# Graph and mixture-of-experts network on one Trainium2 core: TensorE turns the next group's rows ahead of this group's logits

## The chip, the cores and the metric

The kernel runs on 1 core of a Trainium2 chip. The metric is the device time of one execution in microseconds; of several runs the median is given. The engines are named as in the profile: PE is TensorE's matmul side and PEld its weight loads, DVE is VectorE, ACT is ScalarE, POOL is GpSimd, SP is SyncE.

## The reference

Two layers, each a graph attention network beside a mixing network, and then a feed-forward network of experts, on 6250 rows of 256 features with 106,250 edges, all in float32. The change lies in the last step, the feed-forward network of the second layer:

```python
x = x + _L1_ffn_ref(_layernorm(x, axis=-1)[None], L1_ffn_W1, L1_ffn_b1, L1_ffn_Wg, L1_ffn_bg, L1_ffn_Wd, L1_ffn_bd)[0]

def _L1_ffn_ref(x, W1, b1, Wg, bg, Wd, bd):      # C = 256, HID = 1024, E = 8
    H = jax.nn.gelu(xf @ W1 + b1, approximate=False)
    probs = jax.nn.softmax((H @ Wg + bg) / TEMP, axis=-1)
    assign = jnp.argmax(probs, axis=-1)
    for e in range(Wd.shape[0]):
        y = H @ Wd[e] + bd[e]
        sel = (assign == e)[:, None]
        out = out + jnp.where(sel, probs[:, e:e + 1] * y, 0.0)
```

So every row gets a hidden vector H (1024 wide), eight logits out of it, and the output of the one expert with the largest logit.

## The kernel before

The kernel is written engine by engine: each engine has its own queue of instructions in a fixed order, and the queues meet only in semaphores. Three graph stages ("layers" in the kernel's own count, the third being the second half of the second graph network) take most of the time. Behind the third come the two stages of the last feed-forward network:

- **Routing** (`route_tensor`, `route_scalar`, `route_vector`, `route_gpsimd`, `route_sync`). The 6250 rows lie in SBUF as 49 blocks of 128, the last one padded. They are taken in 13 groups (`GROUPS`): twelve of four blocks and one of a single block. For each group the kernel computes H for all rows only to get the logits, chooses the expert, counts the place of each row in its expert's list, and GpSimd writes the rows to a table in HBM, sorted by expert (`D_sx`).
- **Experts** (`ffn1_tensor` and its siblings). Rows come back from that table in 15 groups, 14 of them full, are turned (L2505), go through W1 (L2513) and through their expert's matrix (L2494).

TensorE wants its left operand with the contraction on the partitions, so rows must be turned (transposed) before a matmul with W1, and the logits, which come out as 8 x 512, must be turned back to rows x 8 before VectorE can take a maximum over eight experts.

The routing is a pipeline over rounds r = 0 to 14. In round r, PE's queue holds, in this order:

1. L2203: the hidden layer of group g = r - 1. Eight slices of 128 hidden units, two matmuls each (k = 0, 1); a float32 matmul shows as two instructions in the profile, hence 32. The results go in turn to four PSUM banks, 2 to 5, and PE waits for ACT's gelu (L2265) of four slices before. It waits first until ACT has copied the turned rows of the whole group (`r_xT`).
2. L2208 and L2209: the counts for group r - 2, when DVE has its choice (`r_hot`).
3. L2215: the logits of group g, 8 x 512 into bank 6, when all gelus are there (`r_h`).
4. L2221: the logits are turned into bank 7, one small transpose a block. Before that PE waits for `r_log` (DVE's L2389 has added the bias to the logits and written them to SBUF) and for `r_taken` (DVE has read the counts of the group before out of bank 7).
5. L2231: the normalised rows of group r are turned, two transposes a block, into banks 0 and 1 in turn. PE waits for `r_xn` (DVE's L419 has normalised the block) and, from the third block on, for `r_xT` of two blocks before (ACT's L2273 has copied it out of the bank).

ACT's queue in a round: the exponential of the logits of group r - 2 (L2248, when DVE has subtracted the maximum, L2311), a copy of that group's rows to a staging tile (L2252), in rounds 1 and 3 a square root for the norm (L2239), eight gelus for group r - 1 (L2265), four copies of turned rows for group r (L2273). Between exponential and gelu its tables are loaded anew, and these loads are shown under the line that follows.

DVE's queue in a round: the choice for group r - 2 (L2307 to L2329: copy out of bank 7, maximum, subtract it, then after the exponential the sum, the probability, the index), in rounds 0 to 2 a part of the `join` that adds the third graph stage's result to the rows (L2282 to L2286: 8, 18 and 19 blocks), the rows of group r (L419), the place of the rows of group r - 2 (L2338 to L2357), and last the bias for group r - 1 (L2389).

GpSimd writes four blocks of rows a round (L2183), when `placed` has given the positions.

Of the kernel before, what the change touches and what calls it, by code (L numbers as in the profile page):

```python
# [32 lines left out]
GROUPS = [(4 * g, 4) for g in range(12)] + [(48, 1)]  # L33
# [86 lines left out]
def program(nc, A, out):  # L120
    ctx = ExitStack()
    with ctx:
        def sb(name, shape, dt=F32):
            return ctx.enter_context(nc.sbuf_tensor(name, shape, dt))
# [11 lines left out]
        def late_sem(name):  # L136

            return early.pop() if early else sem(name)
# [7 lines left out]
        ident = sb("ident", [128, 128])  # L146
# [15 lines left out]
        banks = [ctx.enter_context(nc.psum_tensor(f"ps{i}", [128, 512], F32)) for i in range(8)]  # L162
# [19 lines left out]
        def meet(e, n):  # L182
            e.drain().then_inc(all_there, 1)
            e.wait_ge(all_there, 5 * n)
# [451 lines left out]
        NGR = len(GROUPS)  # L636
# [1479 lines left out]
        def z2_tensor(e):  # L2116
# [29 lines left out]
        rl = AR.ring(2, 512)  # L2146
# [13 lines left out]
        j_std, r_xn, r_tr, r_xT, r_hps, r_h, r_gps, r_log, r_ltr, r_sub, r_exp, r_hot, r_rank, r_taken, r_pos, r_staged, r_iota = [  # L2160
            late_sem(n) for n in ("j_std", "r_xn", "r_tr", "r_xT", "r_hps", "r_h", "r_gps", "r_log", "r_ltr", "r_sub", "r_exp", "r_hot", "r_rank", "r_taken", "r_pos", "r_staged", "r_iota")]
# [27 lines left out]
        def route_tensor(e):  # L2189
            e.wait_ge(route_in, 96)  # L2190
            for r in range(NGR + 2):
                if 1 <= r < NGR + 1:
                    g = r - 1
                    b0, nb = GROUPS[g]
                    w = 128 * nb
                    xt, h = rxt2[g % 2], rH[g % 2]
                    e.wait_ge(r_xT, b0 + nb)
                    for m in range(8):
                        n = 8 * g + m
                        if n >= 4:  # L2200
                            e.wait_ge(r_h, n - 3)
                        for k in range(2):
                            t = e.matmul(banks[2 + n % 4][:, 0:w], W1[:, k, 128 * m:128 * m + 128], xt[:, k, 0:w], start=(k == 0), stop=(k == 1))  # L2203
                        t.then_inc(r_hps, 1)
                if r >= 2:
                    c = 8 * GROUPS[r - 2][1]
                    e.wait_ge(r_hot, r - 1)
                    e.matmul(banks[7][:, 64:64 + c], tri1[:, :], O1[r % 2][:, 0:c], start=True, stop=True)  # L2208
                    e.matmul(banks[7][:, 96:96 + c], ones1[:, :], O1[r % 2][:, 0:c], start=True, stop=True).then_inc(r_rank, 1)  # L2209
                if 1 <= r < NGR + 1:  # L2210
                    e.wait_ge(r_h, 8 * g + 8)
                    if g:
                        e.wait_ge(r_sub, g)
                    for m in range(8):
                        t = e.matmul(banks[6][0:8, 0:w], Wg[:, m, :], h[:, m, 0:w], start=(m == 0), stop=(m == 7))  # L2215
                    t.then_inc(r_gps, 1)
                    e.wait_ge(r_log, g + 1)
                    if g:
                        e.wait_ge(r_taken, g)
                    for i in range(nb):  # L2220
                        t = e.transpose(banks[7][:, 8 * i:8 * i + 8], rl[g % 2][0:8, 128 * i:128 * i + 128], ident[0:8, 0:8])  # L2221
                    t.then_inc(r_ltr, 1)
                if r < NGR:
                    b0, nb = GROUPS[r]
                    for i in range(nb):
                        b = b0 + i
                        e.wait_ge(r_xn, b + 1)
                        if b >= 2:
                            e.wait_ge(r_xT, b - 1)
                        for k in range(2):  # L2230
                            t = e.transpose(banks[b % 2][:, 128 * k:128 * k + 128], rx3[b % 4][:, 128 * k:128 * k + 128], ident[:, :])  # L2231
                        t.then_inc(r_tr, 1)
            meet(e, 12)

        def route_scalar(e):
# [348 lines left out]
        @block.tensor  # L2584
        def _(e):
            walk = Walk(e, "pe")
            prep_tensor(e)
            mix0a_tensor(e)
            kv0_tensor(e)
            mix0_tensor(e)  # L2590
            stream_tensor(e, L0, walk, Alone())
            meet(e, 5)
            meet(e, 6)
            ffn0_tensor(e, (Walk(e, "pe1"), walk))
            mix1a_tensor(e)
            stream_tensor(e, L1, walk, Out1())
            meet(e, 9)
            z2_tensor(e)
            stream_tensor(e, L2, walk, Alone())
            meet(e, 11)  # L2600
            route_tensor(e)
            ffn1_tensor(e, walk)
# [55 lines left out]
```

## Time and profile before

| | |
|---|---|
| median of 3 runs | 5911.1 us (5902.32 to 5912.36) |
| profiled execution, its own time | 5899.81 us |
| its span, first to last instruction | 5898.0 us |
| mean granted TensorE clock | 0.847 of full speed |
| PE busy in the whole span | 4097.7 us (69%) |
| DVE, ACT, POOL busy | 3502.1, 3190.4, 3221.9 us |
| chain that ended last, L2203 and L2215 | 3% and 1% of the span |

The profile is of one execution. Its times are in microseconds from the span's start. A row of the timeline gives start, length, engine, line, operation, operands and count, and in brackets the idle time before it with the instruction that ended it. Rows of equal instructions are merged. The granted clock is the share of full speed (2.4 GHz) that the chip let TensorE have; 0.5 is its lower level, 1.2 GHz. The ends of matmuls are modelled, and one begins before the end of the one before.

### The profile page before, as it was taken

The page shows a single profiled execution, that of the slowest core. Times are in us where ns is not written, and L with a number is a line of the kernel's source. Part 1 is how long each engine was busy: PE and PEld are TensorE (multiplying, and loading weights), DVE is VectorE, ACT ScalarE, POOL GpSimd, SP SyncE. Part 2 cuts the span into 40 slices and gives each one's busy share as a digit, 9 for nine tenths or more (in the row PEclk, how much of TensorE's full clock was granted, in tenths as well). Part 3 has the DMA queues.
Part 4 walks back from the last instruction along what each step waited for, and adds up shares of the span by engine and source line. Part 5 has one row for each costly group of instructions (what it writes and reads, how often), then busy time and mean ns, then how long its engine had stood idle before and what let it go on. Part 6 is the DMA issues. An engine that isn't in the chain of part 4 may idle for free. (4 is left out here: it accounts for less than half of the span.)

```text
span 5898.0 us, 75019 instructions
## 1 busy us (share of the span) xinstructions
PE 4097.7 (69%) x17699; PEld 2854.2 (48%) x17699; DVE 3502.1 (59%) x10103; ACT 3190.4 (54%) x7093; POOL 3221.9 (55%) x3353
## 2 busy tenths in 40 slices
PE   1976566666661597957788777546666666697998
PEld 1655444444441485646566555334444444333665
DVE  4367666666767535868777777546555555622111
ACT  0355566666661232568888887446666666443222
POOL 0013777777761744377777777257777777111222
PEclk9988788787885598979888998878877778898999
DMA  3093555555541344245444444244444444200110
GB/s 100 33 274 101 139 138 140 141 138 139 142 118 48 106 126 122 76 133 136 127 133 129 129 133 135 66 116 133 134 132 134 133 132 135 80 22 27 33 33 28
DMA packets 347491, 659.77 MB, mean 112 GB/s; under 512 B 78834, under 2 KB 196608, under 8 KB 346664
## 3 DMA queue, kind: packets, MB, share of 16 engines
q0 software_dynamic: 156336, 433.43, 26.9%
q1 hardware_dynamic: 190732, 221.55, 12.8%
q8 instruction: 163, 2.67, 0.2%
q14 instruction: 260, 2.13, 0.1%
HBM read 540.63 MB, written 115.42 MB: 111 GB/s over the span
## 5 line engine op out<-in xcount | busy, mean ns | idle before, releaser
L953 POOL DMA_INDIRECT AR<-D_z,SRCI x1856 | 1763.9, 950 | 789.8 <-issue 506.3
L1178 PE MATMUL ps<-AR 128*128 128x264 f32 (+2 forms) x5568 | 1752.9, 469 | 223.7 <-issue 111.7
L1178 PEld LDWEIGHTS ps<-AR 128*128 128x128 f32 x5568 | 1237.2, 233 | 529.9 <-issue 268.6
L953 POOL DMA_INDIRECT AR<-D_h,SRCI x928 | 894.6, 964 | 283.2 <-issue 246.4
L1225 ACT ACTIVATE AR<-iota_n,NREL 128x128 f32<-128x128 f32 x2784 | 881.2, 389 | 18.5 <-PE ps L1178 11.6
L1044 DVE TENSOR_TENSOR AR<-AR,ps 128x1024 f32<-128x1024 f32 x696 | 836.4, 1202 | 0.0
L1066 DVE TENSOR_TENSOR AR<-ps,AR 128x264 f32 (+2 forms) x1392 | 587.7, 422 | 159.3 <-DVE AR L1066 131.3
L1228 ACT ACTIVATE AR<-AR,ones 128x512 f32<-128x512 f32 x696 | 502.2, 722 | 22.6
L990 DVE TENSOR_TENSOR AR<-AR 128x128 f32<-128x128 f32 (+2 forms) x174 | 48.9, 281 | 749.8 <-SPq L943 748.1
L1149 PE MATMUL ps<-ident,AR 128*128 128x128 f32 (+2 forms) x174 | 60.8, 349 | 614.7 <-DVE AR L992 614.7
L1242 ACT ACTIVATE AR<-ps 128x128 f32<-128x128 f32 (+2 forms) x174 | 46.9, 269 | 710.1 <-PE ps L1149 705.4
L1238 ACT ACTIVATE AR<-AR,ones 128x1024 bf16<-128x1024 bf16 x348 | 399.5, 1148 | 11.3
L1236 ACT ACTIVATE AR<-AR,iota_p 128x1024 bf16<-128x1024 bf16 x348 | 394.5, 1134 | 19.8 <-DMA AR<-D_rel 19.8
L1149 PEld LDWEIGHTS ps<-ident,AR 128*128 128x128 f32 (+2 forms) x174 | 21.4, 123 | 669.5 <-issue 668.0
L1141 PE MATMUL ps<-AD,AR 128*128 x2784 | 197.3, 173 | 110.7 <-issue 50.3
L864 POOL TENSOR_SCALAR AR<-AR 128x512 f32<-128x512 f32 (+1 forms) x26 | 43.3, 1674 | 379.0 <-ACT AR L721 379.0
L2425 POOL DMA_INDIRECT out<-X x57 | 56.8, 997 | 332.7 <-DVE X L2461 319.4
L1141 PEld LDWEIGHTS ps<-AD,AR 128*128 128x128 bf16 x2784 | 141.8, 99 | 199.3 <-issue 165.7
L1250 ACT ACTIVATE AR<-ps 128x128 f32<-128x128 f32 (+2 forms) x174 | 51.3, 295 | 303.5 <-PE ps L1166 301.5
L2494 PE MATMUL ps<-AR 128*128 x912 | 200.8, 381 | 18.2 <-ACT AR L2478 18.2
L2183 POOL DMA_INDIRECT D_sx<-AR x49 | 47.6, 972 | 303.3 <-DVE AR L2357 292.0
L1159 PE MATMUL ps<-ones,AR 1*128 1x1 f32 (+2 forms) x696 | 72.3, 204 | 202.3 <-DVE AR L1025 201.6
(432 smaller groups left out, 7618.7 us busy)
## 6 DMA issues: line engine op xcount, KB each, us to landing
AR<-D_rel SPq DMA_DIRECT2D x348, 256.0 KB
D_sx<-AR SPq DMA_DIRECT2D x8, 6370.0 KB
AR<-D_z,SRCI POOLq DMA_INDIRECT x1856
AR<-D_h,SRCI POOLq DMA_INDIRECT x928
D_y<-AR SPq DMA_DIRECT2D x106, 128.0 KB, 1.7
AR<-in_L_ffn_Wd SPq DMA_DIRECT2D x8, 1024.0 KB, 11.9
AR<-D_mask SPq DMA_DIRECT2D x58, 128.0 KB
D_h<-AR SPq DMA_DIRECT2D x49, 132.0 KB, 1.7
```

The costliest lines, as they stand in the source:

```text
L953: e.indirect_dma_start(out=GV[:, u % 48, :], out_offset=None, in_=D_row[L.i], in_offset=bass.IndirectOffsetOnAxis(ap=SRCI[:, u:u + 1], axi ...
L1044: e.tensor_tensor(G, G, w, ALU.mult).then_inc(m_ready, 1)
L1066: e.tensor_tensor(o, banks[n % 3][:, 0:YW], o, ALU.add).then_inc(slot_added, 1)
L1141: t = e.matmul(BK_AD[:, 3 * H * u:3 * H * u + 3 * H], OHr[v][:, 128 * (u % 8):128 * (u % 8) + 128], AD3[:, at], start=True, stop=True)
L1149: e.transpose(BK_T[0:P, 0:128], AD[:, 0:P], ident[:, :]).then_inc(t_ps, 1)
L1159: t = e.matmul(BK_T[0:P, 384 + i:385 + i], ROW[0:1, i, 0:P], ones[0:1, 0:1], start=True, stop=True)
L1178: t = e.matmul(banks[n % 3][:, 0:YW], Sr[:, u % 8, :], GV[:, u % 48, :], start=(i == 0), stop=(i == 1))
L1225: t = e.activation(w[:, i, :], iota_n[:, :], ACT.Abs, bias=NREL[:, u:u + 1])
L1228: e.activation(w[:, :, :], w[:, :, :], ACT.Relu, bias=ones[:, 0:1], scale=-1.0).then_inc(s_ready, 1)
L1236: e.activation(OHr[v], RBr[n % 2], ACT.Abs, bias=iota_p[:, 0:1], scale=-1.0).then_inc(*ac.up())
L1238: e.activation(OHr[v], OHr[v], ACT.Relu, bias=ones[:, 0:1], scale=-1.0).then_inc(oh_ready, 1)
L2494: t = e.matmul(ps[:, 0:256], rH2[q % 2][:, m, 128 * i:128 * i + 128], Wd[:, m, bass.ds(at, 256)], start=(m == 0), stop=(m == 7))
```

## The change

In `route_tensor`, step 4 (wait for `r_log`, wait for `r_taken`, turn the logits of group g) is taken from its place ahead of step 5 and put behind it. In round r TensorE thus turns the rows of group r first and the logits of group r - 1 after them. The counts that the waits ask for, the operands and the banks are the same; the other engines' queues are untouched. Round 0 has no step 4, and rounds 13 and 14 have no step 5.

```diff
@@ -2214,12 +2214,6 @@
                     for m in range(8):
                         t = e.matmul(banks[6][0:8, 0:w], Wg[:, m, :], h[:, m, 0:w], start=(m == 0), stop=(m == 7))
                     t.then_inc(r_gps, 1)
-                    e.wait_ge(r_log, g + 1)
-                    if g:
-                        e.wait_ge(r_taken, g)
-                    for i in range(nb):
-                        t = e.transpose(banks[7][:, 8 * i:8 * i + 8], rl[g % 2][0:8, 128 * i:128 * i + 128], ident[0:8, 0:8])
-                    t.then_inc(r_ltr, 1)
                 if r < NGR:
                     b0, nb = GROUPS[r]
                     for i in range(nb):
@@ -2230,6 +2224,13 @@
                         for k in range(2):
                             t = e.transpose(banks[b % 2][:, 128 * k:128 * k + 128], rx3[b % 4][:, 128 * k:128 * k + 128], ident[:, :])
                         t.then_inc(r_tr, 1)
+                if 1 <= r < NGR + 1:
+                    e.wait_ge(r_log, g + 1)
+                    if g:
+                        e.wait_ge(r_taken, g)
+                    for i in range(GROUPS[g][1]):
+                        t = e.transpose(banks[7][:, 8 * i:8 * i + 8], rl[g % 2][0:8, 128 * i:128 * i + 128], ident[0:8, 0:8])
+                    t.then_inc(r_ltr, 1)
             meet(e, 12)
```

## Rows read from the trace of the kernel before

**Rows 1.** Busy time by stretch: PE, PEld, DVE, ACT, POOL; granted clock, DMA share, GB/s
```profile
5080.00:5440.00 360.00, 300.94 (x827) 123.01 (x826) 127.14 (x643) 134.72 (x210) 53.73 (x58) 0.91 0.13 44
5440.00:5898.00 458.00, 417.99 (x1500) 272.68 (x1500) 77.16 (x220) 99.11 (x175) 105.96 (x109) 0.99 0.10 31
```

**Rows 2.** Chain that ended last, round 5: start, us, engine, tile, line, count
```profile
5216.21 0.75 DVE AR L2389
5218.85 0.67 ACT AR L2273 x2
5219.56 15.71 PE ps L2203 x32
```

**Rows 3.** Timeline of PE, round 5
```profile
5209.14 7.03 PE L2215 MATMUL ps<-AR 128*8 128x512 f32 x16 [0.41 <-ACT AR L2265]
5217.00 0.41 PE L2221 MATMUL ps<-ident,AR 8*128 8x8 f32 x4 [0.83 <-DVE AR L2389]
5217.34 0.66 PE L2231 MATMUL ps<-ident,AR 128*128 128x128 f32 x4
5218.40 0.69 PE L2231 MATMUL ps<-ident,AR 128*128 128x128 f32 x4 [0.41 <-ACT AR L2273]
5219.56 15.70 PE L2203 MATMUL ps<-AR 128*128 128x512 f32 x32 [0.47 <-ACT AR L2273]
```

**Rows 4.** Timeline of all engines, DVE and ACT at the end of round 5
```profile
5217.45 0.19 DVE L2307 COPY AR<-ps 128x32 f32<-128x32 f32 x1 [0.50 <-PE ps L2221]
...
5217.89 0.19 DVE L2311 TENSOR_TENSOR AR<-AR 128x32 f32<-128x32 f32 x1
...
5219.53 1.28 ACT L2248 ACT_TABLE_LOAD   x1
...
5223.15 1.38 DVE L419 TENSOR_SCALAR AR<-X,MV,RS 128x256 f32<-128x256 f32 x4
```

**Rows 5.** Timeline of PE, L2203 behind the turns of rounds 4, 6 and 10
```profile
5192.88 15.47 PE L2203 MATMUL ps<-AR 128*128 128x512 f32 x32 [0.47 <-ACT AR L2273]
...
5246.46 14.00 PE L2203 MATMUL ps<-AR 128*128 128x512 f32 x32 [0.47 <-ACT AR L2273]
...
5348.98 15.70 PE L2203 MATMUL ps<-AR 128*128 128x512 f32 x32 [0.47 <-ACT AR L2273]
```

**Rows 6.** Busy time by stretch, columns of rows 1, start of L2203 behind round 5
```profile
5219.40:5221.40 2.00, 1.84 (x3) 0.81 (x4) 0.28 (x2) 1.97 (x4) 0.00 (x0) 0.60 0.00 0
5221.40:5223.00 1.60, 1.60 (x4) 0.57 (x3) 1.46 (x15) 0.60 (x1) 0.00 (x0) 0.50 0.00 0
```

**Rows 7.** Timeline of PE in the expert stage, one of 13 like rounds
```profile
5489.78 14.08 PE L2494 MATMUL ps<-AR 128*128 x64 [1.17 <-ACT AR L2478]
5503.70 0.60 PE L2505 MATMUL ps<-ident,X 128*128 128x128 f32 x4
5504.70 0.69 PE L2505 MATMUL ps<-ident,X 128*128 128x128 f32 x4 [0.41 <-ACT AR L2472]
5505.86 14.00 PE L2513 MATMUL ps<-AR 128*128 128x512 f32 x32 [0.47 <-ACT AR L2472]
```

**Rows 8.** Timeline of DVE and PE in rounds 0 and 2
```profile
5078.36 1.38 DVE L419 TENSOR_SCALAR AR<-X,MV,RS 128x256 f32<-128x256 f32 x4
...
5132.79 1.35 DVE L419 TENSOR_SCALAR AR<-X,MV,RS 128x256 f32<-128x256 f32 x4
...
5136.13 0.73 DVE L2389 TENSOR_SCALAR AR<-ps,AR 8x512 f32<-8x512 f32 x1
...
5081.70 16.45 PE L2203 MATMUL ps<-AR 128*128 128x512 f32 x32 [0.47 <-ACT AR L2273]
...
5136.92 0.59 PE L2221 MATMUL ps<-ident,AR 8*128 8x8 f32 x4 [5.81 <-DVE AR L2389]
...
5140.32 16.15 PE L2203 MATMUL ps<-AR 128*128 128x512 f32 x32 [0.47 <-ACT AR L2273]
```

**Rows 9.** Timeline of ACT, round 12
```profile
5399.80 1.28 ACT L2248 ACT_TABLE_LOAD   x1
```

## The prediction

> **What bounds the kernel now.** I read the page first, then the busy time by stretch, the chain of work that ended last, and at the end the timeline of one round, engine by engine. The change touches one stage only, the routing of the last layer; it fills most of the stretch from 5080 to 5440 us. There TensorE (PE) is busy 300.94 of 360 us, while VectorE (DVE), ScalarE (ACT) and GpSimd (POOL) are each busy under 135 us [rows 1]. In the expert stage behind it, PE is busy 418 of 458 us [rows 1]. So PE's queue sets the length of both, and the chain says the same: in a round it runs L2215 (logits), L2389 on DVE, the turns, L2273 on ACT, L2203 (hidden layer of the next group), with no detour over POOL or a DMA [rows 2]. Whatever the change takes out of PE's queue in a round should come off the total, unless something takes its place.
>
> The timeline of round 5 shows what is to be gained [rows 3]. L2215 ends at 5209.14 + 7.03 = 5216.17. PE then waits 0.83 us for DVE's L2389, which adds the bias to the logits (0.75 us, [rows 2]). L2221 turns the logits from 5217.00, and the row turns L2231 begin only at 5217.34. They take two pieces with 0.41 between them, in which ACT copies a block out of PSUM. After the last, PE waits 0.47 us for ACT's copy, and L2203 begins at 5219.56. From the end of L2215 to L2203 that is 3.39 us, of which 0.83 + 0.41 + 0.47 = 1.71 us is idle.
>
> **The clock is the second thing in the stretch.** L2203 has the same 32 instructions in each full round, yet it takes 14.00 us in some rounds and 15.47 to 15.71 in others [rows 2, 3, 5]. I count the L2203 that follows the turns of a round to that round. Of the ten regular rounds (1 and 3 to 11) four have a long one: 4, 5, 9 and 10, with 15.47, 15.70, 15.70 and 15.70 us. The busy table says why: just behind the turns of round 5 the granted clock is 0.60, then 0.50, so PE fell from 2.4 to 1.2 GHz and came back [rows 6]. What it did before was the stretch with 1.71 us of idle time. Over the stage the four falls cost 1.47 + 3 × 1.70 = 6.6 us.
>
> **The change part by part.** Nothing is added or removed: the same transposes, the same waits, no DMA moves. In rounds 1 to 12 the block "wait for r_log, wait for r_taken, turn the logits" goes behind the row turns. Only PE's queue changes its order.
>
> *A regular round.* The row turns wait for r_xn, which DVE gave long before (for round 6 L419 runs from 5223.15 to 5224.53, when the L2203 ahead of that round's logits and turns still has over 10 us to go, [rows 3, 4]), and for ACT's copies. So L2231 can follow L2215 at once. What starting at once looks like is shown by the expert stage, where the same turns (L2505) come behind long matmuls without a wait: L2494 ends at 5489.78 + 14.08 = 5503.86 and L2505 starts at 5503.70, 0.16 before that [rows 7]. L2231 thus moves from 5217.34 to 5216.01, 1.33 us earlier. ACT's copies, and with them L2203, move with it. L2221 now lies behind the last turns, which end 0.47 us ahead of L2203; it takes 0.41 us, or 0.34 from its start to the next one's [rows 3]. It fits beneath the wait for ACT's copy, by 0.06 us. The wait for DVE (L2389 ends 0.79 us after L2215, [rows 2, 3]) lies beneath the turns, which take 1.75 us. So a regular round gets shorter by **1.33 us**. Bounds: if L2221 is not covered at all, 1.33 − 0.34 = 0.99. From above, the expert stage needs 5505.86 − 5503.86 = 2.00 us for the same stretch without logits [rows 7], so 3.39 − 2.00 = 1.39. I take 1.33, since it comes from this stage's own rows. Ten such rounds give 13.3 us.
>
> *What is late next.* L2221 itself comes 0.76 us later against L2215: at 5217.76 in the time of round 5, in place of 5217.00. Behind it stand DVE's L2307 to L2311, 0.89 + 0.19 us after its start, so L2311 would end at 5218.84. ACT needs that for the exponential L2248, but loads its table first: the load ends at 5219.53 + 1.28 = 5220.81 now, 5219.48 after the change [rows 4]. A slack of 0.64 us is left, so ACT and its gelus behind it do not wait. This is the cover of the move; if it were gone, PE would still have the PSUM ring of four banks (L2203 starts its fifth slice only half-way) before it felt it. GpSimd's row writes hang on DVE's placing, and POOL is busy 53.73 of 360 us [rows 1].
>
> *Round 2 is another case.* DVE is late there, since it joins 19 blocks (30 to 48) ahead of its rows and the bias. It ends L2389 at 5136.13 + 0.73 = 5136.86, PE turns the logits at 5136.92 and only then the rows, and L2203 begins at 5140.32 [rows 8]. DVE's work in this round began when round 1's turned logits and exponentials came, so it moves 1.33 us forward: L2389 then ends at 5135.53, and L419, whose rows PE turns, starts at 5132.79 − 1.33 = 5131.46. Round 0 shows how long it takes from L419 to L2203: 5081.70 − 5078.36 = 3.34 us, also at the low clock. The rows are then turned and copied at 5134.80, before DVE gives the bias. So L2221 starts at 5135.59, and L2203 0.52 us later (the step to the next instruction now), at 5136.11: 4.21 us earlier than 5140.32. Of these 1.33 is round 1's; round 2 gives **2.9 us**. PE still stands idle for several us there, so the fall of its clock stays. L2203 took 16.15 us behind it and 16.45 in round 0 [rows 8], which makes the bound ± 0.3 us.
>
> *Round 12* turns one block. The second half of the short L2203 behind it waits for ACT, whose queue is table load, exponential, staging copy, table load, gelu from 5399.80 on [rows 9]. ACT's copy moves with L2231, so 1.33 us again. Behind it, the last logits' turn has no row turns beside it, in either kernel.
>
> Sum without the clock: 10 × 1.33 + 2.9 + 1.33 = **17.5 us** (bounds 11 × 0.99 + 2.6 = 13.5 and 11 × 1.39 + 3.2 = 18.5).
>
> *The falls of the clock.* Does the shorter idle time keep the clock up? The nearest row is the expert stage: its turns leave 0.41 and 0.47 us idle, 0.88 together, once per round, and 13 of 13 full L2513 behind such turns take 14.00 us; the stretch has a granted clock of 0.99 [rows 1, 7]. In the routing, the changed stretch would have about 0.41 + 0.06 + nothing for DVE, some 0.5 us, which is less than what the expert stage bears. On the other end are the stretches with 1.71 us, which fell in 4 of 10. So I take all four falls as gone: **6.6 us** more. Bounds 0 and 6.6.
>
> The Trainium skill ("TensorE: Matmul & The Clock Gate", section "A second HAM failure mode: psum-queue depth-cycling") says that small idle spots between groups of matmuls can by themselves make the clock swing; this trace agrees, with four falls at 1.71 us of idle time. Part 1 of the same page says that the moment of a change of level varies from run to run with where the work lies; by that, the number of falls belongs to one execution, and the second term could be anything between 0 and more than 6.6 us in a timed run.
>
> Together 17.5 + 6.6 = **24.1 us**. The profiled execution took 5899.8 us (span 5898.0), so it would take 5875.7. The three timed runs have a median of 5911.1 and lie between 5902.3 and 5912.4, 2.5 to 12.6 us above the profiled one. Against the median the forecast is 5911.1 − 24.1 = **5887.0 us**.
>
> **The rivals.**
> *A: the falls stay.* The clock falls as often as before, since something other than the 1.2 us of idle time that go brings them. For it: the clock fell in only four of ten like rounds, so this idle time alone does not decide. Against it: rows 7. It gives 5911.1 − 17.5 = 5893.6 us. Chance 0.16.
> *B: the logits' turn is not covered*, because its waits are served in order and the wait for ACT's copy comes only behind it. Against it: 0.47 is more than 0.41; for it: the margin is 0.06. It gives 11 × 0.99 + 2.9 + 6.6 = 20.4, so 5890.7 us. Chance 0.08.
> *C: the change does nothing in a round.* The turns wait for something that came late anyway, such as DVE's rows or the copies. Against it: in the nine regular rounds 3 to 11, DVE's L419 is done while L2203 still runs (5224.5 against 5235.3 in the round of [rows 3, 4]), and ACT's copies follow the turns at once. Only round 2's part and the last would be left, under 4 us: 5907 us. Chance 0.04.
> *D: slower.* The groups' shift in time sets the clock's falls anew, in this stage and in the expert stage, where only the first of 14 full L2513 is long, behind a real pause. Place: L2203 and L2513 behind the turns; price 1.70 us each. From 11 falls more than now the 17.5 us are used up; all 12 + 14 rounds falling would cost 26 × 1.70 − 6.6 = 37.6, thus 5911.1 − 17.5 + 37.6 = 5931 us. Against it: in both stages the idle time at the turns would be at most 0.88 us, and with that no round fell. Chance 0.04.
> The forecast keeps 0.68.
>
> **How the numbers follow.** A measurement of this kernel tells about 0.2% (11.8 us) from no change. The forecast, B and A lie beyond it by 12, 9 and 6 us; the median of three runs moves by some 5 us (the runs lie 10 apart). Of A I count a fifth as within, of the forecast and B a tenth. Faster 0.81, within 0.15, slower 0.04. The range: below, 5902.3 − 25.1 = 5877; above, case A at its lower bound, 5911.1 − 13.5 = 5897.6, and 4 us for the spread: 5901.
>
> **What the profile of the changed kernel would show.** L2231 starts 0.1 to 0.2 us before L2215's end, with no idle time put down to DVE L2389 in rounds 1 and 3 to 11; L2221 stands behind the second piece of L2231; from the end of L2215 to L2203 it is 2.0 to 2.1 us; every L2203 of rounds 3 to 11 takes 14.00 us, and two of these begin 23.9 us apart; in round 2, L2203 follows L2221 at once. ACT's exponential starts right behind its table load. I would be wrong if L2221 pushed L2203 back, if idle time <-DVE L2311 appeared at L2248, or if L2203 still took 15.7 us in some rounds.

## The result

The changed kernel takes 5878.15 us in the median of 6 runs (5866.76 to 5880.92), the kernel before on the same footing 5902.01 us (5894.31 to 5912.36, 6 runs). The ratio is 0.9952, with a 95% interval of 0.9941 to 0.9964: faster by 0.48%, about 28 us (21 to 35 by the interval), and by the two medians 23.9 us. The forecast was faster by 24.1 us, with 5887.0 us as the time. The profiled execution of the changed kernel took 5866.76 us.

First the page of the changed kernel, its first lines and then the part on engines (busy time and share of the span):

```profile
span 5865.0 us, 75019 instructions
...
PE 4112.9 (70%) x17699; PEld 2872.8 (49%) x17699; DVE 3502.6 (60%) x10103; ACT 3189.8 (54%) x7093; POOL 3219.1 (55%) x3353
```

The instruction counts are the same and the shares have hardly moved, so the page alone does not find the change. The stretches do. This is the routing by stretch in the changed kernel, from its first row turn to the first hidden-layer matmul of the expert stage, and then two short stretches at the start of L2203 behind round 5. The columns are those of [rows 1].

```profile
5071.34:5407.78 336.44, 291.36 (x831) 118.29 (x832) 128.69 (x648) 135.27 (x213) 54.41 (x59) 0.94 0.14 47
5202.00:5204.00 2.00, 1.89 (x5) 0.93 (x6) 0.90 (x5) 1.97 (x4) 0.00 (x0) 1.00 0.00 0
5204.00:5205.60 1.60, 1.60 (x5) 0.69 (x4) 1.43 (x16) 1.58 (x2) 0.00 (x0) 1.00 0.00 0
```

The same stretch of the kernel before:

```profile
5078.92:5441.11 362.19, 302.66 (x831) 123.93 (x832) 128.67 (x648) 135.52 (x213) 54.54 (x59) 0.91 0.13 44
```

The same 831 matmul instructions are done in 336.44 us in place of 362.19, 25.75 us less. PE is busy 11.3 us less with them, though no instruction went: nearly all of that is the clock, 0.94 against 0.91. The other 14.4 us are idle time that went. The two short stretches answer to [rows 6]: there the clock was 0.60 and 0.50, now it is 1.00.

The two spans differ by 33.0 us. Of that 7.6 us lie ahead of the routing (its first row turn starts at 5071.34 in place of 5078.92), where both kernels have the same code; 25.75 in the routing; behind it, the changed kernel loses 0.3.

The timeline of PE in round 5 answers to [rows 3]. L2225 are the row turns now (L2231 before), L2232 the logits' turn (L2221 before).

```profile
5192.93 7.03 PE L2215 MATMUL ps<-AR 128*8 128x512 f32 x16 [0.41 <-ACT AR L2266]
5199.89 0.66 PE L2225 MATMUL ps<-ident,AR 128*128 128x128 f32 x4
5200.95 0.68 PE L2225 MATMUL ps<-ident,AR 128*128 128x128 f32 x4 [0.41 <-ACT AR L2274]
5201.57 0.41 PE L2232 MATMUL ps<-ident,AR 8*128 8x8 f32 x4
5202.11 14.00 PE L2203 MATMUL ps<-AR 128*128 128x512 f32 x32
```

The 0.83 us for DVE are gone. L2225 starts 0.07 us before L2215's end (5192.93 + 7.03 = 5199.96), the logits' turn lies in the gap ahead of L2203, and from L2215's end to L2203 it is 2.15 us in place of 3.39: 1.24 us less.

The chain that ended last answers to [rows 2]. DVE's L2389, now L2390, has left it:

```profile
5192.93 7.03 PE ps L2215 x16
5199.96 0.38 PE ps L2225 x2
...
5201.40 0.67 ACT AR L2274 x2
...
5202.11 14.01 PE ps L2203 x32
```

DVE and ACT at the end of round 5 answer to [rows 4]; L2308, L2312 and L2249 stand for L2307, L2311 and L2248:

```profile
5202.01 0.19 DVE L2308 COPY AR<-ps 128x32 f32<-128x32 f32 x1 [1.27 <-PE ps L2232]
5202.08 1.28 ACT L2249 ACT_TABLE_LOAD   x1
...
5202.46 0.19 DVE L2312 TENSOR_TENSOR AR<-AR 128x32 f32<-128x32 f32 x1
5203.37 0.23 ACT L2249 ACTIVATE AR<-AR 128x32 f32<-128x32 f32 x1
```

L2312 ends at 5202.65 and the exponential starts at 5203.37, right behind its table load. So the later turn of the logits makes nobody late; 0.71 us are left.

Round 2 answers to [rows 8]: PE first, then DVE's bias.

```profile
5123.81 0.76 PE L2225 MATMUL ps<-ident,AR 128*128 128x128 f32 x4 [2.12 <-DVE AR L419]
5124.87 0.69 PE L2225 MATMUL ps<-ident,AR 128*128 128x128 f32 x4 [0.30 <-ACT AR L2274]
5127.50 0.59 PE L2232 MATMUL ps<-ident,AR 8*128 8x8 f32 x4 [1.94 <-DVE AR L2390]
5128.02 16.20 PE L2203 MATMUL ps<-AR 128*128 128x512 f32 x32
...
5126.71 0.73 DVE L2390 TENSOR_SCALAR AR<-ps,AR 8x512 f32<-8x512 f32 x1
```

The one wait of 5.81 us has become two, of 2.12 and 1.94, and the rows are turned between them. From the L2203 of round 1 (5099.87) it is 28.15 us to this one, where it was 31.02 (5109.30 to 5140.32): 2.87 less.

### The profile page after: what moved, and what is told of

Read it like the earlier page. It is cut to its first block and busy times, and to the rows that moved or that the text cites. A ratio compares the mean times of both kernels' runs of the same rounds, so it can differ in the third digit from the quotient of the medians.

```text
span 5865.0 us, 75019 instructions
## 1 busy us (share of the span) xinstructions
PE 4112.9 (70%) x17699; PEld 2872.8 (49%) x17699; DVE 3502.6 (60%) x10103; ACT 3189.8 (54%) x7093; POOL 3219.1 (55%) x3353
## 3 DMA queue, kind: packets, MB, share of 16 engines
q14 instruction: 260, 2.13, 0.1%
## 5 line engine op out<-in xcount | busy, mean ns | idle before, releaser
L1178 PE MATMUL ps<-AR 128*128 128x264 f32 (+2 forms) x5568 | 1791.8, 477 | 220.8 <-issue 108.1
L1178 PEld LDWEIGHTS ps<-AR 128*128 128x128 f32 x5568 | 1263.2, 238 | 536.2 <-issue 265.2
L1238 ACT ACTIVATE AR<-AR,ones 128x1024 bf16<-128x1024 bf16 x348 | 399.5, 1148 | 11.3
L2514 PE MATMUL ps<-AR 128*128 128x512 f32 (+1 forms) x480 | 202.1, 579 | 7.2 <-ACT AR L2473 7.2
## 6 DMA issues: line engine op xcount, KB each, us to landing
AR<-in_L_ffn_Wd SPq DMA_DIRECT2D x8, 1024.0 KB, 12.4
```

What stands on the lines that cost most here:

```text
L1178: t = e.matmul(banks[n % 3][:, 0:YW], Sr[:, u % 8, :], GV[:, u % 48, :], start=(i == 0), stop=(i == 1))
L1238: e.activation(OHr[v], OHr[v], ACT.Relu, bias=ones[:, 0:1], scale=-1.0).then_inc(oh_ready, 1)
```

## The experiments

All of them compare the **routing stretch**, from the first row turn to the first full hidden-layer matmul of the expert stage, and the lengths of single rounds in it. There are three sets of runs. The first (the kernel before and the changed kernel once more, the wait, the filled wait) took 5.9 ms a run. In the second (round 2, after_timed, early_defer) and the third (defer_3to11, after_timed2) something slowed the stages ahead of the routing, and every kernel, the one before and the changed one alike, took 6.6 to 6.7 ms, but for one run of the kernel before at 9.26 ms, which the ratios leave out. Their totals are read only as ratios within a set. The totals of the first set are single runs, and those of the kernel before spread over 18 us in the result, so they decide nothing: 5907.60 and 5899.07 us before, 5879.04 changed, 5897.68 with the wait, 5906.57 with the filled wait.

### The kernel before, once more

No edit.

> The kernel before, unchanged, for a second profile. Measured from the first row turn of the routing to the first hidden-layer matmul of the expert stage (362.2 us in the first profile, 336.4 us in that of the changed kernel). Theory (the clock falls where 1.7 us of idle time lie behind the logits, and which rounds it hits depends on how the rounds lie in time): full-speed rounds again last 25.2 us from one L2203 to the next and those with a fall 26.7 to 26.9, three to six of the ten regular rounds have a fall, though perhaps others than 4, 5, 9 and 10, and the stretch is 362 us plus or minus 4. Rival (the falls belong to that one execution): 0 or 1 fall, and about 355 us.

```profile
5243.60 15.70 PE L2203 MATMUL ps<-AR 128*128 128x512 f32 x32 [0.47 <-ACT AR L2273]
5270.50 15.70 PE L2203 MATMUL ps<-AR 128*128 128x512 f32 x32 [0.47 <-ACT AR L2273]
...
5322.60 15.46 PE L2203 MATMUL ps<-AR 128*128 128x512 f32 x32 [0.47 <-ACT AR L2273]
5349.27 15.70 PE L2203 MATMUL ps<-AR 128*128 128x512 f32 x32 [0.47 <-ACT AR L2273]
```

Those are rows of PE's timeline. Four of the ten regular rounds have a fall, as in the first profile, though in rounds 6, 7, 9 and 10 in place of 4, 5, 9 and 10. Rounds without one last 25.20 to 25.21 us. The stretch takes 359.57 us. That some rounds fall belongs to this order of the queue and not to one execution; which ones fall does change.

### The changed kernel, once more

No edit.

> The changed kernel for a second profile. Theory (some 0.6 us of idle time do not bring a fall): all L2203 behind the turns of rounds 1 and 3 to 11 take 14.00 us again, rounds last 23.96 us, and the stretch from the first row turn to the expert stage's first hidden-layer matmul is 336.4 us within 1 us. Rival (the first profile was lucky with where the rounds lay): some of them take 15.5 to 15.7 us, and the stretch is 338 to 345 us.

The ten L2203 behind the turns of rounds 1 and 3 to 11 take 14.00 us, or have the next one 23.96 us behind them where the rows are not merged into one. The stretch takes 336.93 us. With the two timed runs further down (335.70 and 335.77) and the kernel with the new order in all rounds but one, that makes five executions with 50 regular rounds in the new order and not one fall. In the old order it is 13 of 30 (4, 4 and 5 in the round-2 kernel below). The ten rounds of an execution follow each other at an equal step, so they are not ten independent trials.

### The wait ahead of the turns

```diff
                     t.then_inc(r_gps, 1)
+                    e.wait_ge(r_log, g + 1)
```

on the changed kernel.

> The changed order, but PE waits for the biased logits in the old place, ahead of the row turns; the logits are turned behind them as in the changed kernel. So only the cover of the logits' turn is left of the change, and PE has some 0.8 + 0.4 + 0.1 us of idle time behind the logits again. Theory (the wait is the larger part of the 1.24 us gained in a regular round): a round without a fall lasts 23.96 + 0.8 to 0.9 = about 24.8 us, and the clock falls again in some of the ten regular rounds (one to five L2203 over 15 us). Rival A (falls come from the short turns, not from idle time, and left for another reason): no falls. Rival B (the order of the turns is what counts): 24.0 us a round. Round 2 has no gain here beyond about 0.5 us, since DVE's bias comes behind its rows.

```profile
5238.17 7.03 PE L2215 MATMUL ps<-AR 128*8 128x512 f32 x16 [0.41 <-ACT AR L2267]
5246.03 0.66 PE L2226 MATMUL ps<-ident,AR 128*128 128x128 f32 x4 [0.83 <-DVE AR L2391]
5247.10 0.69 PE L2226 MATMUL ps<-ident,AR 128*128 128x128 f32 x4 [0.41 <-ACT AR L2275]
5247.71 0.41 PE L2233 MATMUL ps<-ident,AR 8*128 8x8 f32 x4
5248.25 15.69 PE L2203 MATMUL ps<-AR 128*128 128x512 f32 x32
```

The timeline of PE shows the 0.83 us back, now ahead of the row turns. A round lasts 24.86 us: 0.35 shorter than the old 25.21 by the covered turn of the logits, and 0.90 longer than 23.96. So of the 1.25 us of a regular round, 0.90 are the wait and 0.35 the covered turn. And the falls are back, in three of the ten regular rounds (one of them is shown). Round 2, from L2203 to L2203, takes 30.52 us, 0.5 less than the old 31.02, as expected. The short stretches behind the round shown have the clock at half:

```profile
5248.20:5250.20 2.00, 1.95 (x3) 0.91 (x4) 0.89 (x5) 1.97 (x4) 0.00 (x0) 0.52 0.00 0
5250.20:5251.60 1.40, 1.40 (x3) 0.60 (x2) 1.29 (x14) 0.49 (x1) 0.00 (x0) 0.50 0.00 0
```

The routing stretch is 353.82 us. The order of the turns is the changed kernel's, so the order as such is not what keeps the clock up. Neither rival holds.

### A filled wait in the old order

```diff
                     t.then_inc(r_gps, 1)
+                    e.matmul(banks[2][:, 0:w], W1[:, 0, 0:128], xt[:, 0, 0:w], start=True, stop=True)
                     e.wait_ge(r_log, g + 1)
```

on the kernel before.

> The kernel before, with one superfluous matmul of 128 x 512 put between the logits and the wait for the biased logits (its result is overwritten by the next hidden layer), which keeps PE busy for about 0.86 us where it was idle for 0.83. The order of the turns is that of before, so nothing is gained in the queue. Theory (idle time brings the falls; 0.88 us are left behind it, as in the expert stage): a round lasts 25.2 to 25.4 us, and there are no falls in the ten regular rounds, so L2203 takes 14.00 us in all; the stretch from the first row turn to the expert stage is some 5 to 8 us shorter than that of the kernel before on the same footing. Rival A (the short turns bring the falls): three to five L2203 over 15 us as before, and the stretch 1 us longer than before.

```profile
5244.52 7.03 PE L2215 MATMUL ps<-AR 128*8 128x512 f32 x16 [0.41 <-ACT AR L2266]
5251.48 1.13 PE L2217 MATMUL ps<-AR 128*128 128x512 f32 x2
5252.53 0.41 PE L2222 MATMUL ps<-ident,AR 8*128 8x8 f32 x4
5252.88 0.66 PE L2232 MATMUL ps<-ident,AR 128*128 128x128 f32 x4
5253.94 0.69 PE L2232 MATMUL ps<-ident,AR 128*128 128x128 f32 x4 [0.41 <-ACT AR L2274]
5255.10 14.00 PE L2203 MATMUL ps<-AR 128*128 128x512 f32 x32 [0.47 <-ACT AR L2274]
```

In PE's timeline all ten L2203 take 14.00 us, and rounds last 25.36 us, 0.15 more than the old 25.21. The stretch is 356.80 us, 5.4 and 2.8 us less than the two of the kernel before: **more work on PE, no shortening of the queue, and still a shorter stretch**. This parts the two terms of the sum. The short turns are all there, in the old place, and by themselves do not bring the clock down in a regular round; with the 0.83 us of idle time ahead of them they did. It is one execution. (In round 12, behind a wait of 2.12 us for ACT, the clock did fall for a moment: the second half of the short L2203 took 2.46 us in place of 2.05.) Of the expected "5 to 8 us" one comparison lies within, the other below: a fall costs 1.70 us and is saved, but the added matmul costs some 0.15 us a round.

One rival these runs do not part from idle time. From the end of the last large matmul (L2215, or the added L2217) to L2203, turns and idle time together, it is 3.39 us in the old order and 3.05 with the wait, where the clock fell, and 2.49 with the filled wait, 2.15 in the changed kernel and 2.00 in the expert stage, where it did not. The idle time in these stretches is 1.71, 1.37, 0.88, 0.54 and 0.88 us. Whether it is the idle time alone or the whole stretch without a large matmul that brings the fall down, no run shows; the 0.83 us wait tips the balance by either.

### Round 2 alone, and all rounds but round 2

```diff
                     t.then_inc(r_gps, 1)
+                    if not (r == 2):
+                        e.wait_ge(r_log, g + 1)
...
-                if 1 <= r < NGR + 1:
+                if 1 <= r < NGR + 1 and (r == 2):
                     e.wait_ge(r_log, g + 1)
```

on the changed kernel (shortened; the first block is the old place of the logits' turn, the second the new one), and the same with `r != 2`.

> The new order in round 2 alone, the old one in all other rounds. Theory: from the L2203 behind the turns of round 1 to the one behind round 2 it is 31.0 - 2.9 = about 28.2 us (the step measured 31.02 before and 28.15 in the changed kernel), all other regular rounds 25.2 us or 26.9 with a fall; three to five falls stay. Rival (round 2's gain rests on DVE's being earlier through round 1's new order, and not on its own): 29.5 us or more.

> The new order in all rounds but round 2. Theory: the L2203 of rounds 1 and 2 stand 31.0 us apart as in the kernel before (DVE's bias, then the logits' turn, then the rows), every regular round lasts 23.96 us without a fall, and the stretch from the first row turn to the expert stage is 336.4 + 2.9 = 339.3 us, within 1 us. Rival (round 2 catches up what it loses, because DVE sets the length of the first rounds whatever PE's order): 337 us or less.

PE in round 2, first with the new order there alone (L2232 are the row turns, L2222 and L2239 the logits' turn in its old and its new place):

```profile
5889.28 0.76 PE L2232 MATMUL ps<-ident,AR 128*128 128x128 f32 x4 [0.43 <-DVE AR L419]
...
5892.98 0.59 PE L2239 MATMUL ps<-ident,AR 8*128 8x8 f32 x4 [1.95 <-DVE AR L2397]
5893.50 17.04 PE L2203 MATMUL ps<-AR 128*128 128x512 f32 x32
```

and then with the old order there alone:

```profile
5907.73 0.59 PE L2222 MATMUL ps<-ident,AR 8*128 8x8 f32 x4 [5.83 <-DVE AR L2397]
...
5911.12 16.12 PE L2203 MATMUL ps<-AR 128*128 128x512 f32 x32 [0.47 <-ACT AR L2281]
```

From L2203 to L2203 it is 28.16 us in the first (from 5865.34) and 31.03 in the second (from 5880.09), so round 2 is worth 2.87 us on its own, whatever the other rounds do. In the first of the two the L2203 that begins the step had a fall (15.70 us) and the step was no longer: PE waits 0.43 us for DVE's rows in place of 2.12, so here DVE sets the length, and the new order only takes the turns from behind its bias. Without round 2, the stretch takes 338.91 us; with it, 335.70 in the same set of runs: the difference of 3.2 is the 2.87 and 0.27 by which the L2203 behind round 2 took longer (16.12 against 15.85). The round-2 kernel's stretch is 358.47 us. It keeps 25.2 us a round, and has falls in five of its ten regular rounds.

### Further along the same way

In rounds from 3 on, PE turns the first two blocks ahead of the wait for the last gelu and the other two amid the logits. In every round it turns a group's logits only behind the first slice of the next group's hidden layer. The edit is to the kernel before; the lines that matter (`turn_rows` and `turn_logits` hold the old waits and transposes):

```diff
+                        if True and m == 0 and g >= 1:
+                            turn_logits(g - 1)
...
+                    if r not in (1, 2):
+                        for b in rows[0:2]:
+                            turn_rows(b)
+                        rows = rows[2:]
                     e.wait_ge(r_h, 8 * g + 8)
...
                         t = e.matmul(banks[6][0:8, 0:w], Wg[:, m, :], h[:, m, 0:w], start=(m == 0), stop=(m == 7))
+                        if m == 3 and r not in (1, 2):
+                            for b in rows:
+                                turn_rows(b)
+                            rows = []
```

> A version that goes further: from round 3 on PE turns the first two blocks of rows ahead of the wait for the last gelu, the other two in the middle of the logits' eight steps, and the logits of a group only behind the first slice of the next group's hidden layer. PE then has none of the three waits of the changed kernel (0.41 for the gelu, 0.41 and about 0.5 for copies). Theory (PE's queue alone sets the round): a regular round lasts 22.9 to 23.1 us in place of 23.96, and the stretch from the first row turn to the expert stage is 9 to 10 us shorter than 336.4, so 326 to 328 us; total ratio to the kernel before 0.994. Rival (the choice of experts has no slack left: the logits' turn comes 2 us later, so ACT's exponential and its gelus behind it come late, and PE waits for a bank at the fifth slice): 23.9 us or more a round, with idle time ahead of L2203's later slices, and no gain over the changed kernel.

A regular round lasts 22.96 us, and PE has no idle time in it at all. But the stretch is 330.79 us, not 326 to 328. By PE's timeline, two parts are longer than in the changed kernel of the same set of runs: from round 0's L2203 to round 1's it is 26.22 us against 25.08, and from round 11's to the expert stage 64.3 against 62.1. (The hidden layer is L2220 in this kernel and the next, the exponential L2263, and DVE's subtraction of the maximum L2326.) In round 12 ACT waits for DVE's late L2326 ahead of the short group's gelus (timeline of ACT), and I took this wait for the cause of the second part:

```profile
6154.50 0.23 ACT L2263 ACTIVATE AR<-AR 128x32 f32<-128x32 f32 x1 [7.37 <-DVE AR L2326]
```

The next kernel keeps the late turn of the logits for rounds 3 to 11 alone:

```diff
-                        if True and m == 0 and g >= 1:
+                        if m == 0 and 3 <= g < NGR - 1:
                             turn_logits(g - 1)
```

> As early_defer, but the logits' turn goes behind the next group's first slice only in rounds 3 to 11; in rounds 1, 2 and 12 it keeps its place at the end of the round. Theory (in early_defer the regular rounds took 22.96 us as expected, but the later turn cost about 1.1 us in round 1, where DVE's joins wait behind the choice, and about 2.6 us in round 12, where ACT's exponential stands ahead of the short group's gelus): the stretch from the first row turn to the expert stage is 326.5 to 328 us, 3 to 4 us shorter than the 330.8 of early_defer and 8 to 10 shorter than that of the changed kernel. Rival (those microseconds were lost to the clock's phase in the first rounds): 330 us or more. Total ratio to the kernel before: 0.9935 to 0.9945.

> The changed kernel against the one before, timed on one chip. Its routing is 22.6 to 25.7 us shorter in the profiles so far (362.2 and 359.6 us before, 336.4 and 336.9 after), and nothing else differs, so both theories expect a ratio of 0.9955 to 0.9965. A rival, by which the totals also carry a gain ahead of or behind the stage, expects 0.9945 or less.

> The changed kernel once more, on the same chip and with the same runs of the kernel before as defer_3to11. The stretch from the first row turn to the expert stage: 335.7 to 337 us, no L2203 over 14.1 us behind the turns of rounds 1 and 3 to 11. Ratio 0.995 to 0.9965, and defer_3to11 lies below it by 0.001 to 0.002.

The stretch of defer_3to11 is **328.03 us**, at the edge of the 326.5 to 328 that were expected. It is 7.7 us less than the changed kernel's 335.77 in the same set, a little under the expected 8 to 10. Of the 2.8 us that it gains on early_defer, 1.95 lie behind round 11 (62.3 us now) and 0.8 in rounds 2 and 3.

The 1.95 us are not the lateness that the theory blamed. ACT's wait of 7.37 us stands in this kernel too, and the second half of the short L2220 begins 27.23 us after round 11's L2220 in both. What differs comes behind that. First PE in early_defer, then ACT and PE in defer_3to11:

```profile
6157.43 3.38 PE L2220 MATMUL ps<-AR 128*128 128x128 f32 x16 [2.11 <-ACT AR L2280]
```

```profile
6155.75 0.23 ACT L2263 ACTIVATE AR<-AR 128x32 f32<-128x32 f32 x1 [7.37 <-DVE AR L2326]
6158.68 2.05 PE L2220 MATMUL ps<-AR 128*128 128x128 f32 x16 [1.66 <-ACT AR L2280]
```

In early_defer the granted clock was 0.62 and then 0.50 there, in defer_3to11 it was 1.00. Up to the next logits that makes 1.47 us; the other 0.5 lie in the plan behind the routing. At this place the clock fell in some kernels and not in others behind the same wait of 2.12 us (2.46 us for the half with the filled wait, 2.05 with the wait ahead of the turns), so whether the later turn had a part in this fall is not shown.

The 1.1 us of round 1 did not come back: it is 26.19 us from round 0's L2220 to the next. I had laid them to DVE's joins, and that was wrong. They lie in the first hidden layer itself, which takes 16.3 us in both of these kernels and 15.2 and 15.3 in the profiles of after_timed and after_timed2, so in how long the clock stays low behind the pause ahead of the routing; there the rival was right. Against after_timed2 this alone is 1.0 us that defer_3to11 lacks. The changed kernel's stretches (335.70 and 335.77 us) and the ratio of after_timed (0.996) came as expected; that of after_timed2 (0.9967) lies just above its range, and defer_3to11 lies 0.0025 below it where 0.001 to 0.002 were expected, all with intervals wider than these differences. Seven rounds of defer_3to11 from L2220 to L2220, by stretch, read PE busy all the time:

```profile
5970.70:6131.45 160.75, 160.75 (x450) 62.11 (x449) 45.11 (x273) 72.47 (x112) 27.15 (x28) 1.00 0.07 24
```

ACT does wait, 4.7 us a round, for the later logits, as the rival of early_defer said, but its gelus have that to spare; behind their table load (the second row), four of the eight still wait 1.03 us each for PE's slices:

```profile
5996.70 0.23 ACT L2263 ACTIVATE AR<-AR 128x32 f32<-128x32 f32 x1 [4.72 <-DVE AR L2326]
...
5997.92 1.28 ACT L2280 ACT_TABLE_LOAD   x1
```

| kernel | routing stretch, us | ratio of the total to before (95%) |
|---|---|---|
| before | 362.19, 359.57 | |
| changed | 336.44, 336.93, 335.70, 335.77 | 0.9952 (0.9941 to 0.9964); 0.996 (0.9942 to 0.9979); 0.9967 (0.9939 to 0.9995) |
| early_defer | 330.79 | 0.994 (0.9923 to 0.9958) |
| defer_3to11 | 328.03 | 0.9942 (0.9914 to 0.9969) |

By the totals, the last two cannot be told apart, nor surely from the changed kernel; by their stretches they can. That the 7.7 us reach the total is likely, since PE's queue sets both, but the intervals do not show it.

## Why the prediction was right, and where it was not

**What bounds the stage**: right for the regular rounds, in every kernel: whatever left PE's queue came off the round, one for one. In round 2 DVE sets the length, as the prediction had it, and in round 12 ACT.

**The regular round**: 1.33 us forecast, 1.24 measured (3.39 to 2.15). The term rested on L2231 starting 0.16 us before L2215's end, as L2505 does in the expert stage [rows 7]; it starts 0.07 before. The logits' turn is covered, as forecast: of the ten rounds' 12.4 us, the wait is about 9.0 and the cover about 3.4, by the wait kernel. Rival B is out.

**Round 2**: 2.9 forecast, 2.87 measured, twice. Both the mechanism (DVE's bias stays last, the rows move beneath it) and the time were read off [rows 8].

**Round 12**: mis-sized, since I read ACT's side of it and passed by PE's. From the L2203 of round 11 to the first count matmul (L2208) of the last round it was 37.2 us and is 34.3. Beside the 1.3 us forecast (1.25 measured, up to the second half of the short L2203) there was one more fall of the clock. It shows in the short L2203 of the kernel before, and is gone after:

```profile
5404.01 3.71 PE L2203 MATMUL ps<-AR 128*128 128x128 f32 x16 [1.12 <-ACT AR L2265]
```

```profile
5372.77 2.05 PE L2203 MATMUL ps<-AR 128*128 128x128 f32 x16 [1.84 <-ACT AR L2266]
```

That is 1.66 us which the sum lacked, though [rows 9] stand right beside it. It belongs to the one execution. In the second profile of the kernel before the clock fell in the first half, and the wait for ACT hid it; the second half begins 28.1 us after round 11's L2203 in both:

```profile
5400.13 3.31 PE L2203 MATMUL ps<-AR 128*128 128x128 f32 x16 [0.53 <-ACT AR L2273]
5404.30 2.05 PE L2203 MATMUL ps<-AR 128*128 128x128 f32 x16 [0.85 <-ACT AR L2265]
```

**The falls**: right in size (4 falls, 6.57 us, all gone), and in cause as far as the runs go. The step from the expert stage's 0.88 us of idle time without falls to this stage's 0.5 held, and two kernels, one execution each, set the idle time and the order apart: 0.83 us put back brings falls back, 0.83 us filled with useless work takes them away. Rival A is out. The number of falls hardly moved between three executions in the old order (4, 4, 5); which rounds fell did. That idle time as such counts, and not the whole stretch without a large matmul, stays open. By the Trainium skill ("TensorE: Matmul & The Clock Gate", section "A second HAM failure mode: psum-queue depth-cycling") small idle spots between groups can make the clock swing; the trace agrees, with three falls in ten rounds at 0.83 + 0.41 + 0.13 us, none in ten at 0.41 + 0.47 (the filled wait) and none in fifty at 0.41 + 0.13.

**The sum in the stretch**: 12.4 + 2.9 + 1.25 + 6.6 + 1.6 is 24.7; with 0.6 from a shorter low-clock start in round 0 (16.45 to 15.84 us) and 0.4 in the plan behind the routing, it comes to the measured 25.75. Forecast 24.1. Against the second profile of the kernel before, where the first L2203 took 15.86 us and the 1.66 were hidden, it is 23.1.

**The time itself** is where the prediction failed: 5887.0 against 5878.15. Against the 5902.0 of the kernel before, that is 15 us faster, where the ratio gives 28. The step that failed is the last one, from the sum to the time, "against the median". I took 24.1 us off 5911.1, the median of three runs, and noted that the profiled execution lay 11.3 us below it without drawing anything from that. The median of six runs is 5902.01; 24.1 off that is 5877.9, within 0.3 us of the result; so close is luck, since the ratio's interval alone is 14 us wide. Most of what differs from run to run is not in the routing. Its stretch repeats within 1.3 us for the changed kernel (four profiles, 335.70 to 336.93) and 2.6 for the one before (two profiles), while its first row turn came between 5071 and 5090 us in six profiles of 5.9 ms, with the same code ahead of it. So most of the spread of the totals, 18 us over six runs before, comes from what stands ahead of the routing, and the three runs at hand were a high draw. The low end, 5877, left 1.2 us below the measured median, too little: it was reckoned from the lowest of the three runs as if none could lie below (the profiled ones of both kernels do).

**The rivals.** A (falls stay) and B (no cover) are out. C (nothing happens in a round) is out. D (slower, by falls elsewhere) did not come: the 13 full hidden layers of the expert stage behind its first take 14.00 us in the changed kernel too, and from the first L2513 to the end it is 456.9 us before and 457.2 after.

## What to carry to other kernels

When the queue of the engine that bounds a stage waits for a short answer from another (here PE for a bias of 0.75 us), put the next independent piece of the same queue in between: it cost nothing here, and the consumer of the answer tells how late it may come. On TensorE count such a wait twice, as its own length and as what it may do to the clock: here 0.83 us of idle time among short transposes cost, beyond itself, some 1.7 us in four or five rounds of ten. And set the sum against more than one anchor: here the change could be read off its stage to 1 or 2 us, while the median of three totals missed that of six by 9.

## What the runs showed that was not expected

- **A useless matmul made the kernel's routing faster**: 356.80 us with it against 362.19 and 359.57 without, since PE did not go idle in that wait and L2203 kept its 14.00 us in all ten regular rounds. The single total, 5906.57 us, shows no gain.
- **Two more microseconds of lateness for the logits cost nothing in the regular rounds and 0.8 us in rounds 2 and 3**, where DVE has 19 blocks to join behind the choice (PE's wait for its rows, L419, is 3.36 us in early_defer and 2.13 in defer_3to11). The 1.95 us at the other end, which looked like the same, were in the main a fall of the clock.
- **The same kernel took 5.87 to 5.88 ms in the runs of the result and the first set, and 6.63 to 6.72 ms in the two others**, while its routing took 336 to 337 us in all. What slowed the stages ahead of it, no run here was made to show.
